# Two-layer graph network on one core: written-out programs for the end of the edge stage, and a reordered last stage

## The reference, cut to what matters

```
r = concat(x1[src], x1[dst], edge) @ Wr.T + br
q = x1 @ Wq.T + bq ;  k = r @ Wk.T + bk ;  v = r @ Wv.T + bv        (8 heads of 64)
a = <q[dst], k> / 8 ;  attn = softmax of a over the edges of one dst
u = x1 + segment_sum(v * attn, dst) @ Wo.T + bo
u = (u - mean) * rsqrt(var + eps) * gamma + beta      (mean, var over all nodes, per feature)
out = LayerNorm(x1 + u)                               (per node)
```

## Time and profile before

| | us |
|---|---|
| median of 3 runs (1485.9 to 1490.85) | 1487.54 |
| the profiled execution | 1490.75 |
| its span in the profile | 1489.0 |
| DVE busy | 1114.7 (75%) |
| PE busy | 1338.8 (90%) |
| POOL busy | 830.7 (56%) |
| ACT busy | 597.8 (40%) |

### The profile page before, as it was taken

The page is one execution under the profiler, slowest core; times in us unless marked ns, Lnnn a source line. Parts: engine busy times, 40 slices in busy tenths (PEclk is TensorE's granted clock), DMA queues, the critical chain, the costliest instruction groups (busy, mean ns, idle before and its releaser), DMA issues. The chain is left out here.

```text
span 1489.0 us, 25046 instructions
## 1 busy us (share of the span) xinstructions
PE 1338.8 (90%) x7872; PEld 1133.1 (76%) x7872; DVE 1114.7 (75%) x1975; ACT 597.8 (40%) x1116; POOL 830.7 (56%) x804
## 2 busy tenths in 40 slices
PE   1899978999999769999999999999999996377877
PEld 1899976888878659999999999999999985333333
DVE  5566636888888714678888888888888887577776
ACT  1576643555555512232223322222232222346565
POOL 2777715666666524555555555556555543356664
PEclk9999998999999979999999999999999997689998
DMA  3799745666666431534445444444444435598544
GB/s 122 231 312 319 256 175 201 221 221 217 223 217 222 148 132 58 150 112 139 136 132 161 134 130 127 127 127 127 127 127 127 127 114 191 167 321 274 192 150 158
DMA packets 123096, 258.97 MB, mean 174 GB/s; under 512 B 20859, under 2 KB 21307, under 8 KB 122914
## 3 DMA queue, kind: packets, MB, share of 16 engines
q1 hardware_dynamic: 92578, 176.90, 36.5%
q0 software_dynamic: 29920, 80.38, 17.5%
q10 hardware_dynamic: 544, 1.05, 0.2%
HBM read 198.23 MB, written 73.61 MB: 183 GB/s over the span
## 5 line engine op out<-in xcount | busy, mean ns | idle before, releaser
L174 PE MATMUL pse<-w_lo,w_hi 128*128 128x256 f32 (+1 forms) x1440 | 467.9, 325 | 25.3 <-DVE w_lo L1154 19.8
L175 PE MATMUL pse<-w_hi,w_lo 128*128 128x256 f32 (+1 forms) x1440 | 463.0, 322 | 0.0
L176 PE MATMUL pse<-w_hi 128*128 128x256 f32 (+1 forms) x1440 | 462.7, 321 | 0.0
L174 PEld LDWEIGHTS pse<-w_lo,w_hi 128*128 128x128 f32 x1440 | 277.3, 193 | 47.5 <-issue 22.2
L176 PEld LDWEIGHTS pse<-w_hi 128*128 128x128 f32 x1440 | 277.2, 192 | 20.1
L175 PEld LDWEIGHTS pse<-w_hi,w_lo 128*128 128x128 f32 x1440 | 277.7, 193 | 18.6
L985 POOL TENSOR_TENSOR acc_x<-acc_x,node_rows 128x512 f32<-128x512 f32 (+1 forms) x79 | 125.5, 1589 | 73.3 <-DMA node_rows<-x_table 68.7
L711 POOL TENSOR_TENSOR node_y<-node_z,node_x 128x512 f32<-128x512 f32 x79 | 101.9, 1290 | 101.4 <-issue 80.1
L174 PE MATMUL psn<-w_lo,agg_hi 128*128 128x512 f32 x316 | 125.7, 398 | 0.0
L175 PE MATMUL psn<-w_hi,agg_lo 128*128 128x512 f32 x316 | 125.7, 398 | 0.0
L176 PE MATMUL psn<-w_hi,agg_hi 128*128 128x512 f32 x316 | 125.6, 398 | 0.0
(11 more groups left out here) (221 smaller groups left out, 2882.8 us busy)
## 6 DMA issues: line engine op xcount, KB each, us to landing
coef_all<-coef_table SPq DMA_DIRECT2D x40, 512.0 KB, 7.0
node_x<-in_x SPq DMA_DIRECT2D x79, 256.0 KB, 2.7
x_table<-node_x SPq DMA_DIRECT2D x79, 256.0 KB, 2.0
node_rows<-x_table SPq DMA_DIRECT2D x79, 256.0 KB, 7.0
edge_part<-part SPq DMA_DIRECT2D x20, 512.0 KB, 3.6
sum_table<-sums SPq DMA_DIRECT2D x40, 256.0 KB, 5.0
part_in<-edge_part SPq DMA_DIRECT2D x20, 512.0 KB
msg_table<-dst_rows_and_msg SPq DMA_DIRECT2D x40, 256.0 KB, 3.6
```

Source lines behind the costliest of these rows:

```text
L174: pe.matmul(to, left[0], right[1], start=first, stop=False)
L175: pe.matmul(to, left[1], right[0], start=False, stop=False)
L176: return pe.matmul(to, left[0], right[0], start=False, stop=last)
```

## The change

**Edge stage.** `sweep` gets `tail=False`: it ends after step 19. All five engines then have a program of their own for what is left (Z = 19 is the last block). What differs in it from the steps 20 to 23 of before:

- TensorE: `turn_scores(18)` stands in the middle of the product r of block 19 and not behind it; the keys of block 19 come ahead of v as before, and `turn_scores(19)` stands in the middle of v and no longer waits for the sums of squares; the messages of block 18 go to `ps_qk`.
- GpSimd multiplies k by q for block 19 (VectorE did so before, L1124). It issues all six late gathers in one run, to three pairs of buffers and without copies of the indices, and it takes over the squares of the last seven node tiles (subtracted from `sum_xx`; VectorE added them to `acc_xx`).
- The coefficients of block 19 aren't stored and read back: GpSimd makes a selection matrix of 8 x 512 (two `affine_select`), and four float32 products put the coefficients on all partitions in PSUM (`wide`). The weighting, the running sum, its split and the product by Wo of block 19 go column part by column part.
- VectorE mixes the four running sums of block 17 with the work on r and q of block 19. The rows of blocks 17, 18 and 19 go to three buffers of their own.
- SP loads the first four groups of x1 tiles right after r of block 19, ahead of the coefficients of block 18 and of the last node tiles.

```diff
+                pe.wait_ge(x_lo, 4 * NB)
+                pe.wait_ge(v_ok, K * Z)
+                by_columns([WR_SRC, WR_DST], left_x, range(0, 2))
+                turn_scores(Z - 1)
+                by_columns([WR_SRC, WR_DST], left_x, range(2, K)).then_inc(r_mm, 1)
+                for q in range(2):
+                    queries(Z, q)
+                pe.wait_ge(r_lo, NB)
+                for q in range(2):
+                    keys(Z, q)
+                by_columns([WV], left_r, range(0, 2))
+                turn_scores(Z)
+                by_columns([WV], left_r, range(2, K)).then_inc(v_mm, 1)
+                for q in range(2):
+                    messages(Z - 2, q)
+                pe.wait_ge(init_ok, 5)
+                pe.wait_ge(cp_ok, NB)
+                for m in range(K):
+                    if m == 2:
+                        pe.wait_ge(v_ok, K * NB)
+                    pe.matmul(wide[m][:], pick[:, m, :], expo[:].rearrange("h c e -> h (c e)"), start=True, stop=True).then_inc(coef_wide, 1)
+                pe.wait_ge(s_lo, Z)
+                pe.wait_ge(k_ok, 2 * NB)
+                for q in range(2):
+                    by_rows(late_o[1][q][:], lambda k: [h[:, k, q * P:(q + 1) * P] for h in st], WO).then_inc(o_mm, 1)
+                pe.wait_ge(uu_added, 2 * (Z - 1))
+                for k in range(K):
+                    pe.wait_ge(s_lo, Z + k + 1)
+                    for q in range(2):
+                        mm = g.product(pe, late_o[2][q][:], [h[:, k, q * P:(q + 1) * P] for h in rt], [g.w(h, WO, k) for h in (g.w_hi, g.w_lo)], k == 0, k == K - 1)
...
+                maxima(Z - 1, (Z - 1) % 2)
+                weigh_v(Z - 2, Z % 2)
+                scan_v(Z % 2, 0)
+                add_part(Z, Z % 2)
+                scan_v(Z % 2, 1)
+                r_low(Z, Z % 2)
+                add_q(Z, 0)
+                scan_v(Z % 2, 2)
+                add_q(Z, 1)
+                scan_v(Z % 2, 3)
+                keep_carry(Z - 2, Z % 2)
+                coefficients(Z - 1, (Z - 1) % 2)
+                for q in range(2):
+                    add_k(Z, q)
+                sum_low(Z - 2, Z % 2)
+                for q in range(2):
+                    sum_scores(Z, q)
+                maxima(Z, Z % 2)
+                weigh_v(Z - 1, (Z - 1) % 2)
+                coefficients(Z, Z % 2)
+                for m in range(K):
+                    scan_v((Z - 1) % 2, m)
+                keep_carry(Z - 1, (Z - 1) % 2)
+                late_rows(0, 0)
+                sum_low(Z - 1, (Z - 1) % 2)
+                late_rows(0, 1)
+                for q in range(2):
+                    add_sum_squares(Z - 2, q, late_o[0])
...
+                for m in range(K):
+                    to = vt[:, Z % 2, m, :]
+                    dve.wait_ge(coef_wide, m + 1)
+                    v.tensor_tensor(to, to, wide[m][:, BE:], ALU.mult).then_inc(mul_ok, 1)
+                    dve.wait_ge(mul_ok, 2 * Z + m + 1)
+                    v.tensor_tensor_scan(to, wide[m][:, 0:BE], to, carry[:, m:m + 1], ALU.mult, ALU.add).then_inc(scan_ok, 1)
+                    if m >= 1:
+                        last_low(m - 1)
+                last_low(K - 1)
+                for i in (1, 2):
+                    for q in range(2):
+                        late_rows(i, q)
+                for i in (1, 2):
+                    for q in range(2):
+                        add_sum_squares(Z - 2 + i, q, late_o[i])
```

GpSimd's program for the same stretch, and SP's order:

```diff
+                weigh(Z - 1)
+                add_nodes(Z - 1)
+                add_dst_squares(Z - 3, again, SN * (Z - 1))
...
+                weigh(Z)
+                take_node_squares(Z - 1, 2 * (Z - 2))
+                add_nodes(Z)
+                take_node_squares(Z, 2 * (Z - 2))
+                for i in range(3):
+                    add_dst_squares(Z - 2 + i, late[i], NT)
...
+                store_u(Z - 3)
+                sp.wait_ge(r_mm, NB)
+                for i in range(4):
+                    load_x1(nc, g, i)
...
+                sp.wait_ge(q_mm, 2 * NB)
+                for i in range(4, 6):
+                    load_x1(nc, g, i)
+                sp.wait_ge(sq_added, SN * Z)
+                for q in range(NT - SN * Z):
+                    sp.dma_start(node[:, q, :], g.x1_table[(SN * Z + q) * P:(SN * Z + q + 1) * P, :]).then_inc(node_in, 16)
+                for b in range(Z - 2, NB):
+                    store_u(b)
```

```diff
-    PAIR, NORM = 8, 11
+    PAIR, NORM = 8, 10
+    ADD = 4
...
-                    j = k - 5
+                    j = k - ADD
                     if j >= 0 and by_pool(j):
...
-                for i in range(2):
-                    pe.wait_ge(spread_ok, i + 1)
-                    pe.matmul(ps[1 + i][:], g.ones[:], spread[:, i, :, :].rearrange("p k n -> p (k n)"), start=True, stop=True).then_inc(wide_ok, 1)
-                pe.wait_ge(coef_ok, 1)
+                pe.wait_ge(split_ok, 3)
+                pe.wait_ge(rows_ok, K)
+                pe.matmul(scale[:], ones_r[:], scale_hi[:].rearrange("p k n -> p (k n)"), start=True, stop=False)
+                pe.matmul(scale[:], ones_r[:], scale_lo[:].rearrange("p k n -> p (k n)"), start=False, stop=True).then_inc(wide_ok, 1)
...
+                for k in range(K):
+                    dve.wait_ge(rows_ok, K + k + 1)
+                    v.scalar_tensor_tensor(shift[:, k, :], mirror[:], lo_turned[:, k:k + 1], shift_hi[:, k, :], ALU.mult, ALU.add).then_inc(shift_ok, 1)
+                dve.wait_ge(wide_ok, 1)
...
-                    done = k - 5
+                    done = k - 6
...
-                    j = k - 2
+                    j = k - 3
...
-                        v.scalar_tensor_tensor(bias[:, m:m + n, :], mv[:, m:m + n, 0:1], -1.0, rstd[:, m:m + n, :], ALU.mult, ALU.mult).then_inc(scale_ok, 1)
+                        for i in range(m, m + n):
+                            v.tensor_scalar(bias[:, i, :], mv[:, i, 0:1], rstd[:, i, :], -1.0, ALU.mult, ALU.mult).then_inc(scale_ok, 1)
```

355 lines of the change are left out of this document (249 added, 106 removed).

## The result

| | before | after |
|---|---|---|
| median of 5 runs, us | 1489.28 (1485.9 to 1490.85) | 1473.19 (1472.64 to 1477.53) |
| ratio, 95% interval | | 0.9902 [0.989, 0.9915] |
| profiled execution / its span, us | 1490.75 / 1489.0 | 1474.68 / 1472.9 |
| granted clock, mean | 0.962 | 0.967 |

The account below looks back on a forecast made before the run. A chain of waits bounds the edge stage's end, VectorE with held biases the loop. Edge -18.5, prologue -2.6, early loop +2.2, later loop -9.2 make -28.1 us: median 1459.4, own range 1451 to 1466, cases 1449 to 1472.

Parts of the forecast that it names:

- Edge stage: End of the edge stage: new orders bring the last stage's start from 1295.56 to 1277.1, -18.5 us (-11 to -22).
- 2 us late at worst: Edge stage: 4 MB of x1 loads issued 11 us ahead delay block 18's coefficients by at most 2 us.
- clock: Edge stage: TensorE idles ahead of the messages of block 18 and runs them slower, 1.9 us added (0 to 4.5).
- Prologue: Start of the last stage, first spreading product to first scaling: cheaper spreading of the factor, -2.6 us (-1 to -3.5).
- Loop, the bias: Last stage's loop: biases no longer held by GpSimd's addition, eight tiles 16.3 instead of 17.86 us, -9.2 over 47 tiles.
- the bias is still held: Rival, loop: GpSimd holds the tensor_scalar too, eight tiles keep 17.86 us or more, whole 1468.6; chance 0.10.
- Loop, the order: Loop: bias to next dependent scaling goes from six iterations to four, felt only in the first 32 tiles, +2.2 us.
- 3.6 + L: Loop: time from a bias over copy, gather and landing L to scaling, statistics and next bias; 9.5 at L = 5.9.
- The gathers don't press: Second rival, loop: gathers land in near 4 us, so the first part also runs at 2.04 a tile, 1454; chance 0.25.
- the edge stage gives less: Rival: x1 loads ahead of block 18's coefficients and TensorE at its lower level; 10 us gained, 1468 to 1470; chance 0.13.
- The rival on the other side of zero: Slower, loop: four-iteration ring with late gathers; at L = 7 in all 79 tiles 2.65 us each and 1499; chance 0.03.
- the second ring: Loop: bias over addition and TensorE to a tile's statistics, three iterations before and after, claimed to change nothing.

Follow-up runs that it names:

- Experiment 7: Changed kernel with the first four groups of x1 loads issued behind the coefficients of block 18; 1511.2 us, ratio 0.9909 to the kernel before.
- best A: Number 11, changed kernel: write k-11, pair finished k-5, two x1 groups before coefficients of block 18, four behind late node tiles; 1436.99 us, ratio 0.965.
- experiment 1: Changed kernel with the old loop lags put back (write k-11, addition and pair k-5), new bias kept; 1490.33 us, ratio 0.9775 to the kernel before.
- experiment 3: Changed kernel without the x1 loads issued within the loop (tiles from 48 on add old rows); 1490.35 us, ratio 0.9788 to the kernel before.
- 5: The changed kernel itself, repeated on the first chip as control; 1508.96 us, ratio 0.990 to the kernel before.
- experiment 6: Kernel before with only the bias edit, one tensor_scalar a tile; 1510.56 us, ratio 0.9895 to the kernel before.
- 4: Changed kernel with ScalarE's write at k-11 instead of k-10; 1482.91 us, ratio 0.9736 to the kernel before.
- 8: Changed kernel with the write at k-11 and the pair finished at k-5; 1474.19 us, ratio 0.9665 to the kernel before.
- 10: Changed kernel with ScalarE's write at k-12 and the new lags otherwise; 1443.45 us, ratio 0.9692 to the kernel before.
- 12: Best B: as best A, with two more x1 groups in the edge stage, all six held until k and v are done; 1437.86 us, ratio 0.9662.

## Why the prediction was right and wrong

**Edge stage: right in its reason, right in its size by luck.** -18.6 against -18.5. The reason given holds: scores of the last block that no longer stand behind squares and messages come 22.0 us earlier (1238.65 against 1260.67). VectorE's timeline, cut at the prediction's own steps, shows that the sum came out although its terms did not:

| VectorE, us | forecast | measured |
|---|---|---|
| to the coefficients of block 18 | 22.9 | 23.0 |
| to the `maxima` of block 19 | 7.7 | 9.5 |
| to the coefficients of block 19 | 6.5 | 10.1 |
| running sums of block 18 and carry | 5.9 | 2.8 |
| rows, low part and squares of block 17 | 5.2 | 5.8 |
| last block's column parts | 8.4 | 7.7 |
| rows and squares of blocks 18 and 19 | 8.8 | 8.4 |
| clock | 1.9 | no wait |
| barrier | 1.4 | 1.2 |

Too small were the scores of block 19, where VectorE waited 1.17, 0.54 and 0.48 us for GpSimd's products and the turning, and "2 us late at worst" for the coefficients behind 4 MB of x1 loads: I took the loads as gone within 11 us at the full rate, but the store alone took 7 us and VectorE stood 5.25 us, over the 3 us at which I said that I would be wrong. Too large were the holds that I had put on the running sums and the carry, which did not come (2.66 us for the four sums and 0.17 for the carry), and the 1.9 us for the clock: VectorE found the messages of block 18 ready. Some 6 us stand on either side. TensorE waited 4.0 us for coefficients, under the 5 that I had set as a mark:

```profile
PE pse L1508 <- DVE expo L1205: 4.0, 1, 4.0
```

The same program for this stretch took 68.1 to 73.1 us in nine traces (the change's own and eight of the table), so the agreement to 0.1 us is chance. Experiment 7 alone would say that the wait for coefficients can't be taken away with profit; best A shows that it can, if the node rows don't have to wait behind all the x1 loads instead.

**Prologue: right.** 11.26 to 11.28 us in every trace with the new one, 13.89 to 13.91 with the old. ScalarE's eight diagonals, which no row of before had, took 0.32 us each (2.54 for eight), where 0.3 was taken.

**Loop, the bias: right.** The forecast 16.3 us for eight tiles came as 16.1 to 16.2, 16.5 in two last eights (after, experiments 1, 3, 5 and 6), and the edit alone in the kernel before is worth 16 us. The rival "the bias is still held" is out: 79 biases of at most 214 ns, and the same in experiment 6. The rule of the Trainium skill ("SBUF — State Buffer", section "Who interferes with whom") that a `tensor_scalar` may be held by GpSimd had no case here; with one column per partition it never was.

**Loop, the order: wrong, and this is the step that failed.** I had the mechanism: "from a bias to the next scaling that depends on it, six iterations become four", and each turn 3.6 + L. I priced it with L = 5.9, the *median* landing in the earlier trace rows, for 24 tiles, and got +2.2 us. That is the term that was mis-sized, twice over. The ring does not wait for the median gather. It waits for one gather in four, and each of those goes out just ahead of a 1 MB load and takes 6.5 to 7.1 us: (3.6 + 7.0) / 4 = 2.65 us a tile, and the tiles 16 to 39 ran at 2.6 to 2.8. And the pressed tiles were counted to 31, while the loads of the loop go out until GpSimd is at tile 37; the ring stayed slow up to tile 39. The rule that issues the loads stands in the kernel's text, and the earlier trace rows has a median where the ring asks for particular gathers. No run moved the loads against the gathers, so that part rests on the dates and on experiment 3. (In one of the six turns, from the scaling of tile 29 to that of tile 33, the chain runs through TensorE at the lower level of its clock, 1351.6 to 1358.4, and the turn takes 11.5 us.) The ledger:

| | forecast | measured |
|---|---|---|
| first 32 tiles | 68.6 | 73.6 |
| fifth eight | 16.3 | 20.8 |
| last scaling to the end (the reordered lags) | 9.8 | 11.9 |

5.0 + 4.5 + 2.1 = 11.6, and the 38 tiles between came 0.4 us better than forecast: 11.2, the loop's miss (+4.2 against -7.0). With the 1.0 us of the unedited part, and less the 0.2 us by which the edge stage came out better (18.63 against 18.46), it makes the 12.0 us by which the profiled execution (1474.68) missed its forecast (1462.7). Against the same program with the old lags (experiment 1) the order costs 16.2 us of loop and 1.25% of the ratio. The +2.2 us of the sum is not to be held against that, for it has the gain of the bias edit in these tiles already in it; by the second rival's "2.2 less and 4 more" the prediction priced the order at 6.2 us.

**How the parts add up.** By ratio on their own chips: the edge part alone -14 us, the bias alone -16, the prologue -2.6 by its stretch; together some -33, each known to 2 to 4 us. Everything but the new order, experiment 1, gives 0.9775, -34. The whole change gives -16. The difference, 17 to 18 us, is the new order.

**The rivals.** "The gathers don't press" is refuted: they press more than I had it. That the edge stage gives less (10 us) is refuted for the stretch, although its mechanism, x1 loads ahead of the coefficients, is there. The rival on the other side of zero had the right mechanism, the right formula and, with L = 7 and 2.65 us a tile, the right turn, but needed all 79 tiles pressed; some 32 were.

**What the second ring did, which I had as unchanged.** From a bias by the gather, GpSimd's addition behind it, TensorE and the statistics it is three iterations, before and after, and a fourth to the next bias, since only every second iteration makes one. The chain of waits late in the changed loop goes round it:

```profile
1428.41 0.08 DVE fin_bias L1758
...
1431.96 1.00 POOL rows_over_w_lo L1624
...
1432.98 1.28 POOL rows_over_w_lo L1630
...
1434.31 1.14 PE psf L1659 x2
...
1436.22 0.08 DVE fin_bias L1758
```

This turn takes 7.81 us and the next, to the bias at 1444.60, 8.38: 16.19 us for the two, each of four tiles, which is the 16.2 us for eight. No gather's landing is in it, only GpSimd's time to issue one or two gathers (0.6 to 1.0 us each) ahead of an addition. Writing one iteration later moves ScalarE's copy, and with it the gather, away from the addition behind it, and the late eights come to about 14. How the chain runs then was not followed. The kernels with three iterations up to the statistics (after, experiments 1, 3 and 6) have 16.1 to 16.2, those with four (4) or five (8, 10, 11, 12) have about 14 from tile 48 on, where TensorE is full; that floor hides what four and five would differ by. I had seen that ring, called it unchanged and never asked what it was worth to lengthen it.

## What to carry to other kernels

In a loop whose engines run in an order written out by hand, count for each engine the iterations from its output to its own next input that depends on it; that count times the period must cover the way between. Price the way by the transfers that stand in the ring, not by the median of all: a ring of four iterations and a load issued every four iterations meet in every turn. Where buffers allow, one iteration more of slack was worth 25 us of loop here and cost little at its end: from the last scaling to the end of the span it took 11.95, 11.80 and 12.39 us with the write at 10, 11 and 12. Before a combined change is judged by its sum, run its halves: here the edge part alone gave the whole gain, and the last stage's edits had gained and lost some 17 us among themselves.

## What the runs showed of the hardware

- A small store behind large loads in one queue waits for them: 16 KB took 7.0 us behind 4 MB issued 8 to 11 us before (6.2 to 8.1 in nine traces), and 1.5 us without them (experiment 7) or behind 2 MB issued 10 to 11 us before (best A).
- A gather of message rows that takes 2.9 us in the median from tile 40 on took 5.5 in the tiles 16 to 39, beside 1 MB loads. The six issued 0.5 us ahead of such a load took 6.5 to 7.1 us and landed 0.2 to 0.9 us before it did.
- How often a small operation of VectorE with two SBUF inputs is held for GpSimd depends on how the two loops are phased: the same bias instruction took 695 ns in the mean in one order and 447 in the other, with the same greatest value of 1.99 us. A held one can begin ahead of the addition and ends with it: 1369.25 to 1371.24 against 1369.92 to 1371.20. GpSimd was issuing a gather (1368.90 to 1369.90 in the same trace) when it began.
- One column of `tensor_scalar` took 195 to 214 ns in all 79 cases beside the same additions.
- Starved of work, TensorE was also granted less clock: over the same 129 matmuls 0.88 in the 73.6 us of the slow tiles (59.3 us busy) against 0.96 in 61.9 us with the old lags (54.4 us busy).
